# A decoder layer on one core: first loads, early projections, the last join and the routing's first row step put in another order

## The reference

```python
x = x + attn(layernorm(x))            # causal, 16 heads, "line" features of 6 numbers
x = x + xattn(layernorm(x), ctx, ctx) # 16 heads of 16, 1601 keys
x = x + ffn(layernorm(x))             # 16 experts, each takes its 64 best tokens

# attn: q1,q2 from [x, x_prev]; k1,k2 from x; lines(p1,p2) = 6 products differences, normalised
#       softmax(q . (k J^T) / sqrt(6)) @ (x Wv^T + bv), then Wo, bo
# ffn:  logits = (x gate^T) / exp(log_temp)
for _ in range(6):                    # sinkhorn
    t = t - logsumexp(t, over tokens); t = t - logsumexp(t, over experts)
gates, idx = top_k(exp(t), 64)        # per expert
out[idx] += gates * (gelu(x[idx] @ w1 + b1) @ w2 + b2)
```

## Time and profile before

| what | us |
|---|---|
| median of 3 runs | 1168.75 |
| the three runs | 1164.27, 1168.75, 1169.23 |
| the profiled execution | 1163.39 |
| its span, first to last instruction | 1161.4 |
| PE busy in the span | 1093.6 (94%) |
| DVE busy | 855.7 (74%) |
| ACT busy | 721.7 (62%) |

### The profile page before, as it was taken

One profiled execution on the slowest core, in us unless ns is written; L12 is line 12 of the kernel. 1 busy time (PEld: TensorE's weight loads), 2 busy tenths in 40 slices (PEclk: granted clock), 3 DMA queues, 4 the chain that ended last, 5 costly groups with the idle time before them and its releaser, 6 DMA issues.

```text
span 1161.4 us, 30371 instructions
## 1 busy us (share of the span) xinstructions
PE 1093.6 (94%) x12606; PEld 518.9 (45%) x12606; DVE 855.7 (74%) x1997; ACT 721.7 (62%) x835; POOL 145.7 (13%) x253
## 2 busy tenths in 40 slices
PE   4787999999999999999999999999999999878997
PEld 2443433332432333544454455555554553457554
DVE  4888566387778888889788889788887892268621
ACT  0345567887687877677776887677885779520111
POOL 3025125112111011000001000010000000000222
PEclk9898999999999999999999999999999999999999
DMA  5113407832011000103231301111102100088596
GB/s 170 32 36 97 118 17 132 182 46 75 16 39 46 16 16 4 52 27 89 77 105 59 95 16 30 53 48 31 30 5 68 30 17 3 19 282 226 192 349 166
DMA packets 79241, 90.24 MB, mean 78 GB/s; under 512 B 16016, under 2 KB 71632, under 8 KB 79104
## 3 DMA queue, kind: packets, MB, share of 16 engines
q1 hardware_dynamic: 73200, 79.91, 23.9%
q10 hardware_dynamic: 4368, 6.29, 1.8%
q0 software_dynamic: 1536, 2.10, 1.0%
HBM read 73.36 MB, written 14.91 MB: 76 GB/s over the span
## 4 chain that ended last, share of the span: by engine, by line
PE 83%; DVE 9%; issue 3%; ACT 3%; POOL 1%; DMA 1%; ACTq 0%; DVEq 0%
PE po L1795 25%; PE g L1903 16%; PE scores L1771 15%; PE scores L1775 6%; PE g L1888 3%; PE g L1848 2%; PE g L2000 2%; PE g L2024 2%; ACT probs L1202 2%; PE g L1878 1%; PE g L1838 1%; DVE mx L1473 1%; PE g L1894 1%; PE g L1882 1%; PE scores L1804 1%
## 5 line engine op out<-in xcount | busy, mean ns | idle before, releaser
L1202 ACT ACTIVATE probs<-scores 128x1024 f32<-128x1024 f32 (+2 forms) x736 | 676.9, 968 | 234.9 <-PE scores L1771 131.3
L1473 DVE TENSOR_REDUCE mx<-g 128x1 f32<-128x400 f32 (+1 forms) x1024 | 526.1, 568 | 81.9 <-PE g L1903 72.1
L1903 PE MATMUL g<-cross_region,even_region 96*32 96x400 bf16 (+1 forms) x4096 | 307.3, 336 | 0.4
L1771 PE MATMUL scores<-even_region,cross_region 99*32 99x512 bf16 (+1 forms) x3264 | 254.3, 379 | 2.5 <-ACT probs L1202 2.5
L1795 PE MATMUL po<-probs,cross_region 128*32 128x512 f32 (+1 forms) x1664 | 225.0, 594 | 0.8 <-ACT probs L1202 0.8
L1903 PEld LDWEIGHTS g<-cross_region,even_region 96*32 96x32 bf16 x4096 | 121.4, 95 | 182.3 <-DVE mx L1473 79.3
L1795 PE MATMUL po<-probs,self_region 128*32 128x512 f32 (+3 forms) x1280 | 150.2, 543 | 5.6 <-POOL probs L1065 5.0
L1771 PEld LDWEIGHTS scores<-even_region,cross_region 99*32 99x32 bf16 (+1 forms) x3264 | 99.7, 96 | 97.1 <-issue 42.7
L1775 PE MATMUL scores<-self_region 36*128 36x512 bf16 (+3 forms) x640 | 103.5, 356 | 7.6 <-ACT probs L1202 7.3
L1065 POOL TENSOR_SCALAR_AFFINE_SELECT probs<-probs 128x256 f32<-128x256 f32 x128 | 60.8, 484 | 269.5 <-ACT probs L1202 268.6
L1032 POOL TENSOR_TENSOR rstd<-mv,half 128x1 f32<-128x1 f32 x48 | 26.6, 555 | 516.4 <-DVE mv L1281 516.2
(11 more groups left out here) (295 smaller groups left out, 870.2 us busy)
## 6 DMA issues: line engine op xcount, KB each, us to landing
cross_region<-in_w SPq DMA_DIRECT2D x16, 1024.0 KB, 12.8
even_region<-xq_d SPq DMA_DIRECT2D x192, 64.0 KB, 2.3
self_region<-in_w ACTq DMA_DIRECT2D x6, 1024.0 KB, 6.6
self_region<-in_w SPq DMA_DIRECT2D x6, 1024.0 KB, 13.0
cross_region<-xk_d SPq DMA_DIRECT2D x24, 200.1 KB, 8.3
xb<-in_x SPq DMA_DIRECT2D x32, 128.0 KB, 2.8
xb<-x_d SPq DMA_DIRECT2D x32, 128.0 KB, 2.2
probs<-in_w SPq DMA_DIRECT2D x4, 1024.0 KB, 13.3
```

The lines of the kernel that those rows point to most:

```text
L1202: act.activation(probs[0:rows, s % 4, :, off:], ps[s % 2][0:rows, :, off:], ACT.Exp, scale=LSCALE if QUADS[n][0] == "self" else 1.0).then_ ...
L1473: dve.reduce_max(mx[:, k % 2, b, h, c:c + 1], g[:, 0:n_keys], AX_X).then_inc(g_free, 1)
L1771: mm = pe.matmul(ps[s % 2][c:c + n_keys, a, :], k_cross[0:NS * DH + 3, h, i * P + c:i * P + c + n_keys], rhs, start=True, stop=True)
L1903: mm = pe.matmul(g[q:q + 32, 0:n_keys], q_max[k % 2][0:NS * DH, h, b * P + q:b * P + q + 32], k_cross[0:NS * DH, 4 * (k % 4) + h, start:st ...
```

## The change

1. SP asks for the first two x blocks ahead of the weights `w_self`, which are asked for in one DMA as before, then for the other two. The planner is told that these weights land at 8.5.
2. In each group of four blocks (`prep`) only two `stats` stand ahead of the first norm, the others between the norms.
3. The copy that spreads the value bias over columns (`attn_t` from `bv_col`) moves from DVE's start to behind the first tile's `carry_out`.
4. In the last join, `out_proj` of the next block stands ahead of `x_turn` of the block before, and each `gate` comes one turn later.
5. The first three steps of the routing's rows (scale, row maximum, subtraction), their exponential and their sum are done for blocks 0 to 11 while the last quads of attention run; blocks 12 to 15 follow after the last gate.
6. Nine weights of the planner's table have new values, and with the new costs the whole order is another.

```diff
-W = dict(hungry=0.2498, fed=0.0083, act_near=0.2255, max=0.4357, max_ahead=0.0147, max_from=72.59, max_end=10.0224,
+W = dict(hungry=0.2496, fed=0.0083, act_near=0.2255, max=0.1307, max_ahead=0.0147, max_from=72.59, max_end=10.0224,
...
     def prep(j):
-        s = [("x_load", "prep", b, u) for b, u in use] + [("stats", "prep", b, u) for b, u in use] + [("carry", j)]
+        s = [("x_load", "prep", b, u) for b, u in use] + [("stats", "prep", b, u) for b, u in use[:2]] + [("carry", j)]
         for n, (b, u) in enumerate(use):
             s += [("norm", "prep", b, u)]
             if n >= 2:
                 s += [("project", use[n - 2][0])]
             s += [("x_turn", "prep", b, u)]
+            if n + 2 < len(use):
+                s += [("stats", "prep", *use[n + 2])]
...
-                s += [("norm", kind, *three), ("x_turn", kind, *three)] if three else []
+                s += [("norm", kind, *three)] if three else []
                 s += [("out_proj", kind, *two)] if two else []
-                s += [("gate", three[0])] if three else []
-            return s
+                s += [("x_turn", kind, *three)] if three else []
+                s += [("gate", use[n - 3][0])] if n >= 3 else []
+            return s + [("gate", use[-1][0])]
...
         if kind == "project":
-            return [("PE", 2.3, [("x_turn", loads_of["prep", b]), ("carry", b // BPT)] + bank, ("proj_pe", b), LAG),
+            return [("PE", 2.3, [("x_turn", loads_of["prep", b]), ("carry", b // BPT), ("self_in",)] + bank, ("proj_pe", b), LAG),
...
+    at["self_in",] = 8.5
+    free["DVE"] = 3.2
...
+        n_rows = last_in["cross", NT - 1, 2]
+        rows_scale, rows_exp, rows_sum = (("scores", n, 0) for n in (n_rows - 8, n_rows - 4, n_rows))
...
-            sp.dma_start(wself_sb[:, :, :], w_self.rearrange("(k p) n -> p k n", p=P)).then_inc(s_w["self"], 16)
...
                 if kind == "x_load":
                     plain_load(step)
+                    if step[3] == 1:
+                        sp.dma_start(wself_sb[:, :, :], w_self.rearrange("(k p) n -> p k n", p=P)
+                                     ).then_inc(s_w["self"], 16)
...
                         act.wait_ge(pv_done, (s - 4) // 2 + 1)
+                    if step == rows_exp:
+                        act.wait_ge(sink_ready, 1)
+                        act.activation(affin[:, 0:TB - BPT, :], sink[:, 0:TB - BPT, :], ACT.Exp).then_inc(sink_act, 1)
...
-            act.wait_ge(sink_ready, 1)
-            act.activation(affin[:, :, :], sink[:, :, :], ACT.Exp).then_inc(sink_act, 1)
             act.wait_ge(sink_ready, 2)
+            act.activation(affin[:, TB - BPT:, :], sink[:, TB - BPT:, :], ACT.Exp).then_inc(sink_act, 1)
+            act.wait_ge(sink_ready, 3)
...
-            dve.wait_ge(s_w["bv"], 16 * DK)
-            dve.tensor_copy(attn_t[:, :, :], bv_col.unsqueeze(2).broadcast_to((P, DK, P))).then_inc(bias_col, 1)
+            def scale_rows(first, last):
+
+                blocks = slice(first, last)
+                wait_freed(dve, *[("gate", b) for b in range(first, last)])
+                link(dve.tensor_scalar(sink[:, blocks, :], logits[:, blocks, :], temp[:, 0:1], None, ALU.mult))
+                link(dve.reduce_max(row[:, blocks], sink[:, blocks, :], AX_X))
+                dve.tensor_tensor(sink[:, blocks, :], sink[:, blocks, :],
+                                  row[:, blocks].unsqueeze(2).broadcast_to((P, last - first, E)),
+                                  ALU.subtract).then_inc(sink_ready, 1)
...
+                if step == rows_scale:
+                    dve.wait_ge(temp_ready, 1)
+                    link(dve.reciprocal(temp[:, 0:1], temp[:, 1:2]))
+                    scale_rows(0, TB - BPT)
+                elif step == rows_sum:
+                    dve.wait_ge(sink_ready, 1)
+                    dve.wait_ge(sink_act, 1)
+                    link(dve.reduce_sum(row[:, 0:TB - BPT], affin[:, 0:TB - BPT, :], AX_X))
...
                     link(dve.tensor_copy(carry[:, :], xn_t[:, :, TILE]))
+                    if step[1] == 0:
+                        dve.wait_ge(s_w["bv"], 16 * DK)
+                        dve.tensor_copy(attn_t[:, :, :], bv_col.unsqueeze(2).broadcast_to((P, DK, P))
+                                        ).then_inc(bias_col, 1)
...
-            wait_freed(dve, *[("gate", b) for b in range(TB)])
-            link(dve.tensor_scalar(sink[:, :, :], logits[:, :, :], temp[:, 0:1], None, ALU.mult))
-
-            link(dve.reduce_max(row, sink[:, :, :], AX_X))
-            dve.tensor_tensor(sink[:, :, :], sink[:, :, :], over_experts(row), ALU.subtract).then_inc(sink_ready, 1)
-            dve.wait_ge(sink_act, 1)
-            link(dve.reduce_sum(row, affin[:, :, :], AX_X))
+            scale_rows(TB - BPT, TB)
+            dve.wait_ge(sink_act, 2)
+            link(dve.reduce_sum(row[:, TB - BPT:], affin[:, TB - BPT:, :], AX_X))
```

12 lines of the change are left out of this document (5 added, 7 removed).

## The result

The changed kernel takes 1152.44 us (median of 4 runs, 1151.05 to 1153.07) against 1167.14 (4 runs, 1164.27 to 1169.23): ratio 0.9887, interval 0.9867 to 0.9906. The forecast was 1161.0. The time lies in the range and the sign was right, but the size was not: 11.1 us from profiled execution to profiled execution (1163.39 to 1152.26), and 14.7 between the medians, where the sum said 5.4.

A forecast was written before the change was run, and what follows sets the result against it. PE's work was taken to bound 224 to 966 us, so only PE's lost time elsewhere could change: early terms -1.4, rows 0, last join -4.0, sum -5.4 from 1166.4, forecast 1161 us, range 1151 to 1169.5.

The forecast's parts named there:

- the first 16 quads as a whole: 65 to 110 us before: 8 us lost by PE instead of 10.4, so -2.4; bounds +3 and -7.
- the stretch behind them: Quad 16 to the maxima, 110 to 224 us before: 10 us lost instead of 7.4, +2.6; bounds -4 and +7.
- the rows at nothing: Routing rows of blocks 0 to 11: 0.75 us saved after the last gate, 0.8 passed on at quad 346; net 0.
- the join's period: Last join, time from norm to norm: 2.55 us instead of 3.88, set by DVE's cycle.
- The start: Up to the first scores: scores 10.2 us earlier, 8.6 us of PE's work not yet done; net -1.6, bounds 0 and -4.
- All three early terms: -1.4: Sum of start (-1.6), first 16 quads (-2.4) and quad 16 to the maxima (+2.6).
- my own sign: Forecast is wrong if the join's period stays above 3.1 or PE's loss ahead of the maxima changes by over 5 us.
- There the time is PE's work: 224 to 966 us: PE busy all but 4.6 of 742 us with the same matmuls, so no change was counted.
- The last join: Final join: period 2.55 instead of 3.88 us, three times, -4.0; bounds -2.4 and -4.4.
- full pay: Rival, chance 0.30: early losses shrink to 5 us each, -7.8, with start -1.6 and join -4.0; 1153 us.
- the losses of 10.4 and 7.4 us: PE's lost time before the change, idle and clock, in 65 to 110 us and in 110 to 224 us.
- The slower rival by masks: Rival, chance 0.06: masks of quads 16 to 47 beside five line parts add 12 to 17 us; 1173 to 1178 us.

The follow-up runs named there:

- the slot copies' two runs: Seven of eight slot copies back on DVE in the changed kernel: 1159.22 us; all eight on ACT in the kernel before: 1171.46 us.
- The kernel with late rows and the new place of `a_turn`: Changed kernel with all routing rows behind the last gate and, in the last join, `a_turn` right behind the previous block's `out_proj`: 1154.22 us, again 1152.87.
- 230 us above: Clock fall at 225 us in the profile of the kernel before with the new table of weights alone, which took 1170.10 us, ratio 1.0013.

## Why the prediction was wrong in size

*Right:* the first projection (9 forecast, 8.99); the slots on ACT as what sets the first scores; the lower clock and idle PE in the first quads (5 us lost counted; in 53 to 63 us PE is busy 7.81 at a clock of 0.66, so 2.2 + 2.7); the first 16 quads as a whole (-2.4 forecast, -2.8 measured, though a second profile, with more lost by the clock, would make it about -1); the stretch behind them (+2.6 forecast, about +2); the rows at nothing; the join's period (2.55 forecast, 2.60 in the mean, though the last two periods were not DVE's alone: `out_proj` waited 0.17 and 0.55 us for ACT's copy).

*Wrong:* two steps, both of which gave the change too little, and one that gave it too much.

- The start, in "All three early terms: -1.4". These three were worth -4.7, of which the start gave -3.7 where -1.6 stood. A slot copy in a row takes 0.91 us and not 1.01, 0.8 us over eight; group 4 to 7's bias row is at 40.45 and not at 41.81 us as I took for unchanged, 1.4. Both inside my bound of -4. By my own sign, PE's loss ahead of the maxima changing by more than 5 us, this was just short of a refutation.
- "There the time is PE's work", from 224 us on, which put that whole stretch at nothing. It gave -2.6: PE waited 9.3 us there before, and now 6.7. My windows skipped 966 to 1001 us, but the 3.4 us of waits there are the same in both kernels. The rest fell from 5.9 to 3.3 us, and in it the waits for exponentials from 2.3 to 1.2 and those behind DVE's shift parts from 1.7 to 0.4. I had read 4.6 us from 224 to 966 and given the order nothing of it.
- The last join gave less, -2.8 where -4.0 stood, and 0.65 of that belongs to the rows; in runs of like clock it is 3.9. The period was right. What I left out is the join's first turns, which took 8.6 us from the copy of the accumulation to the first norm instead of 7.3, at a granted clock of 0.60 instead of 0.77.

That forecast stood on 1166.4 as the middle of before, and the runs of before do spread over two levels of clock. The changed kernel's do so less, which adds 3.6 us to its gain in medians, 14.7 against 11.1 in the pair of profiles. No term of the sum stood for that.

The rival "full pay" had the number, 1153, to which I gave 0.30, but the number was in part luck. It let the losses of 10.4 and 7.4 us shrink to 5 each. Measured, the first went from 9.5 to 6.7 and the second grew from about 7 to 9; its join was 1.2 us too good and its start 2.1 us too poor, and what closes the gap are the waits behind 224 us and the levels of clock, of which it said nothing. The rule of the Trainium skill that I had set beside the count (SBUF — State Buffer, Who interferes with whom) gave -5.4 for the term that measured -2.8, so the plain count of -2.4 was nearer. The trace agrees that masks beside line parts are drawn out (668 against 492 ns, POOL's wait on PE 3.4 against 1.1 us), but the runs without masks show the two orders as far apart in time, so what that rule describes is there and is not shown to be the cause. The slower rival by masks fell: behind the first tile they took 406 ns in the middle and 1193 at most, and PE waited 1.9 us for two of them.

*What stays open:* which single step of the line parts' new places matters was not tried apart; the planner moves some hundred steps together. That the places of the line parts are what counts, and not those of the context's projections beside them, is argued from the slot copies' two runs and not shown.

## What to carry to other kernels

Cut windows at events of the work (the n-th block done), not at times, before comparing what two orders lose, and cut them at the same count as the forecast did: two quads more moved 3 us from one term into another here. An engine that sits idle ahead of the critical step (ACT for 8.44 us here) is where copies of the busiest engine belong, but only if the order puts something useful into the time so freed: the copies alone made the kernel 3.6 to 5.7 us slower, and the order without them was not shown to be worth anything (1159.2 against 1158.2 with the old order). A table of costs and a rule tuned together must be tried together.

## What the runs showed of the chip

- One program on one core can have more than one level of time: on one chip 1164 to 1166 us at a mean granted clock of 0.983 to 0.986, and 1168.5 to 1171.5 at 0.978 or 0.979, in about even shares. On the other chip runs lie between too. The kernel with late rows and the new place of `a_turn` was profiled twice, at 1147.87 us with 0.985 and at 1155.65 with 0.980: its clock lost 11.5 us in the one and 17.4 in the other, with two falls more from 995 to 1005 and from 1055 to 1065 us, of some 3 us each. Falls cost from 1.5 us (the changed kernel at 125 us) to 5.2 (230 us above).
- PE's idle time is the steadier measure: up to quad 16 it is 2.6 to 2.9 us in seven profiles of the new order, while what the clock took there goes from 2.6 to 6.1 us.
- Where later falls of the clock come differs from profile to profile. Without 32 masks, for which PE had waited 1.1 us, the changed kernel was 5 to 6 us faster, 2.6 of it in the last join 900 us later. Whether that is chance or the earlier saving, these runs don't tell: two profiles of the changed kernel itself differ as much, with 3.2 us lost at 125 and 185 us in the one and nothing there in the other.
- PE can be busy 5.00 of 5 us and still run at a clock of 0.50 (230 to 235 us above): busy time alone does not show it.
